# Gated cross-attention layer on one core: another order in the first units of the second phase, and Q and K kept in DRAM in another layout

## What is computed

```python
x = x + tanh(g_xattn) * xattn(layernorm(x), ctx, mask, bias, ...)
x = x + tanh(g_ffn)  * ffn(layernorm(x), ...)

def xattn(h, kv, mask, bias, ln_weight, w_q, w_k, w_v, w_out):
    n = rmsnorm(h) * ln_weight
    q, k, v = n @ w_q.T, kv @ w_k.T, kv @ w_v.T      # 4096 columns each: 32 heads of 128
    s = softmax(where(mask, einsum(q, k) + bias, -inf))   # by batch and head, 128 x 128
    return h + (einsum(where(mask, s, 0), v)) @ w_out.T   # 4096 -> 512

def ffn(y, ...):   # base product 512 x 512, router with 15 outputs, 8 LoRA experts of rank 16
```

## Time and profile before

| | |
|---|---|
| Median of 3 runs | 874.24 us (872.16 to 874.72) |
| Profiled execution | 874.5 us, its span 872.7 us |
| TensorE busy | 840.9 us (96%) |
| VectorE busy | 661.0 us (76%) |
| ScalarE busy | 490.8 us (56%) |
| GpSimd busy | 488.0 us (56%) |
| DMA queue of SyncE | 214.13 MB, 75.7% of 16 engines over the span |
| Mean granted TensorE clock | 0.986 |
| qk_units stores | 128 of 512 KB, 3.2 us to landing (median) |
| qk_units loads | 64 of 1,024 KB, 7.5 us to landing (median) |

### The profile page before, as it was taken

One profiled execution on the slowest core, in us unless ns is written; L12 is line 12 of the kernel. 1 busy time (PEld: TensorE's weight loads), 2 busy tenths in 40 slices (PEclk: granted clock), 3 DMA queues, 4 the chain that ended last, 5 costly groups with the idle time before them and its releaser, 6 DMA issues.

```text
span 872.7 us, 14037 instructions
## 1 busy us (share of the span) xinstructions
PE 840.9 (96%) x4212; PEld 711.0 (81%) x4212; DVE 661.0 (76%) x1172; ACT 490.8 (56%) x1185; POOL 488.0 (56%) x352
## 2 busy tenths in 40 slices
PE   6999999999999998699999999999999999998898
PEld 5887888778888887587888888888888888886786
DVE  6888777886776566466777788988878888798564
ACT  5566666666676654445555555555555555555210
POOL 0353633645456632565766666666666666766522
PEclk9999999999999999899999999999999999998899
DMA  8876777669777795878898888898889889885001
GB/s 293 298 273 244 272 267 262 256 254 359 303 272 281 276 331 177 253 244 265 247 263 267 259 265 259 253 260 250 250 257 261 250 261 250 275 256 175 5 25 73
DMA packets 155393, 214.73 MB, mean 246 GB/s; under 512 B 10960, under 2 KB 109392, under 8 KB 154960
## 3 DMA queue, kind: packets, MB, share of 16 engines
q1 hardware_dynamic: 155344, 214.13, 75.7%
HBM read 128.11 MB, written 85.98 MB: 245 GB/s over the span
## 4 chain that ended last, share of the span: by engine, by line
PE 63%; DVE 13%; DMA 12%; issue 3%; SPq 3%; ACT 3%; POOL 1%; DVEq 0%; ACTq 0%; POOLq 0%
DMA p_rows<-p_blocks 7%; PE Sb L1429 4%; PE Sb L1431 4%; PE Sb L1430 4%; PE Ab L1600 3%; PE Sb L1576 3%; PE Vb L1420 3%; SPq L349 3%; PE Vb L1422 2%; PE Vb L1421 2%; PE Ob L1420 2%; PE Ob L1421 2%; PE Ob L1422 2%; PE Kb L1420 2%; DVE unit_out L959 2%
## 5 line engine op out<-in xcount | busy, mean ns | idle before, releaser
L498 POOL TENSOR_TENSOR w_lo<-w_raw,w_hi 128x1280 fp32r<-128x1280 f32 (+1 forms) x29 | 84.8, 2924 | 121.8 <-ACT w_hi L646 121.8
L542 POOL TENSOR_TENSOR a_rest<-small_a,A_hi 128x512 f32<-128x512 f32 x64 | 83.0, 1297 | 120.0 <-ACT small_a L774 120.0
L780 ACT ACTIVATE p_exp<-s_sb,negmax 128x128 f32<-128x128 f32 x256 | 99.0, 388 | 12.0 <-DVE negmax L1114 11.5
L535 POOL TENSOR_TENSOR bm<-bias,maskneg 128x512 f32<-128x512 f32 x64 | 83.4, 1304 | 19.6 <-DVE s_sb L1120 11.9
L646 ACT ACTIVATE A_hi<-Ab 128x512 fp32r<-128x512 f32 x64 | 38.1, 595 | 96.9 <-PE Ab L1601 96.9
L547 POOL TENSOR_TENSOR P_hl<-pT,P_hl 128x512 fp32r<-128x512 f32 x64 | 83.4, 1302 | 5.0 <-ACT P_hl L646 5.0
L1600 PE MATMUL Ab<-P_hl,V_hi 128*128 128x256 f32 x256 | 65.4, 333 | 15.6 <-POOL P_hl L547 11.4
L646 ACT ACTIVATE U<-Sb 128x512 f32<-128x512 f32 x90 | 53.6, 600 | 41.6 <-PE Sb L1431 41.0
L646 ACT ACTIVATE w_hi<-w_raw 128x512 fp32r<-128x512 f32 (+2 forms) x67 | 60.2, 903 | 22.9 <-PE Kb L1431 7.2
L1429 PE MATMUL Sb<-t_hi,w_lo 128*128 128x512 f32 x180 | 70.5, 392 | 1.2 <-ACT U L646 1.2
L1431 PE MATMUL Sb<-t_hi,w_hi 128*128 128x512 f32 x180 | 70.1, 389 | 0.0
(11 more groups left out here) (300 smaller groups left out, 2705.4 us busy)
## 6 DMA issues: line engine op xcount, KB each, us to landing
qk_units<-unit_out SPq DMA_DIRECT2D x128, 512.0 KB, 3.2
qk<-qk_units SPq DMA_DIRECT2D x64, 1024.0 KB, 7.5
p_rows<-p_blocks SPq DMA_DIRECT2D x64, 256.0 KB, 3.2
pT<-p_rows SPq DMA_DIRECT2D x256, 64.0 KB, 3.7
w_raw<-wqk SPq DMA_DIRECT2D x31, 512.0 KB, 4.2
v_raw<-wv SPq DMA_DIRECT2D x32, 256.0 KB, 4.5
o_raw<-wo SPq DMA_DIRECT2D x32, 256.0 KB, 4.9
stage<-ctxT SPq DMA_DIRECT2D x8, 256.0 KB, 6.1
```

The source lines that it names most:

```text
L498: pool.tensor_tensor(w_lo[:, n % 2, first:5, :], w_raw[:, n % 2, first:5, :], f32(w_hi[:, n % 2, first:5, :]), ALU.subtract).then_inc(w1_l ...
L535: pool.tensor_tensor(bm[:, :, :], bias4[:, q, :, :], maskneg[:, b:b + 1, :].broadcast_to([P, HU, S]), ALU.add).then_inc(bm_done, 1)
L542: pool.tensor_tensor(a_rest[:, :, :], small_a[:, :, :], f32(A_hi[:, r, :, :]), ALU.subtract).then_inc(a_rest_done, 1)
L780: last = act.activation(p_exp[:, i, :], s_sb[:, i, :], ACT.Exp, bias=negmax[:, i:i + 1], accum_out=rowsum[:, i:i + 1])
```

## The change

1. `qk_units` becomes (2·GROUPS, P, BH, 2·HU, 2·S): the batch stands ahead of the columns. A unit's load reads one run of 8 KB per partition instead of eight of 1 KB; a store writes four runs of 1 KB per partition instead of one of 4 KB.
2. SyncE, `first_units`: the loads of units 3, 4 and 5 move ahead of stores and loads of blocks. The V weights' pieces 0 to 2 of group 1 are issued together at its end.
3. SyncE, `group`: V's pieces are issued in units 1 to 4 of a group instead of 2 to 5, the output weights' pieces in units 5, 6, 7 and 0 instead of 6, 7, 0 and 1.
4. ScalarE, `step`: the exponentials go ahead of the weight conversions. In group 0 the V weights' pieces are converted in units 4, 5, 6 and 6 instead of 3 (ahead of unit 4), 4, 5 and 6; GpSimd alike. ScalarE's list for units 1 to 3 has P's high half of unit 0 ahead of V's of unit 2, and the exponentials of unit 3 ahead of V's high half of unit 3.
5. VectorE: V_lo of unit 0 goes ahead of the normalisation of unit 1.
6. TensorE: scores 3 go ahead of V of units 2 and 3, and P·V 0 ahead of V of unit 4.

```diff
--- before.py
+++ after.py
@@ -321,7 +321,7 @@
                 g, p, half = n % G, i % 2, i // 2
                 head = HU // 2 * (g % 2) + p
                 sp.wait_ge(unit_lo_done[i], n + 1)
-                sp.dma_start(qk_units[2 * (g // 2) + half, :, 2 * head + n // G, :, :],
+                sp.dma_start(qk_units[2 * (g // 2) + half, :, :, 2 * head + n // G, :],
                              f32(unit_out[:, i, :]).rearrange("p (b k) -> p b k", b=BH)).then_inc(st[i], 16)
 
             def load_wv(g, q, k):
@@ -354,8 +354,9 @@
                 sp.dma_start(bias4[:, q, :, :], bias[g, :, :, :]).then_inc(ld_bias, 16)
 
             def load_unit(g, b):
-                sp.dma_start(f32(qk[:, b % 2, :, :, :]).rearrange("p h a k -> p (h a) k"),
-                             qk_units[2 * g + b // BH, :, :, b % BH, :]).then_inc(ld_qk[b % 2], 16)
+                sp.dma_start(f32(qk[:, b % 2, :, :, :]).rearrange("p h a k -> p (h a k)"),
+                             qk_units[2 * g + b // BH, :, b % BH, :, :].rearrange("p c k -> p (c k)")).then_inc(
+                                 ld_qk[b % 2], 16)
 
             sp.dma_start(w_raw[:, 0, A11:S1, :], wqk[0, :, 0:2, :]).then_inc(ld_w0[0], 16)
             for k in (B11, B21, B12, B22):
@@ -411,21 +412,21 @@
                     sp.wait_ge(st[i], 16 * (G + 2))
                 sp.wait_ge(scores_done, 1)
                 load_unit(0, 2)
+                sp.wait_ge(scores_done, 2)
+                load_unit(0, 3)
                 store_blocks(0, 0)
                 load_blocks(0, 0)
-                sp.wait_ge(scores_done, 2)
-                load_unit(0, 3)
                 store_blocks(0, 1)
-                load_blocks(0, 1)
                 sp.wait_ge(scores_done, 3)
                 load_unit(0, 4)
+                load_blocks(0, 1)
+                sp.wait_ge(scores_done, 4)
+                load_unit(0, 5)
                 store_blocks(0, 2)
                 load_blocks(0, 2)
                 sp.wait_ge(m_done[4], J(JOBS - 1))
-                load_wv(1, 1, 0)
-                sp.wait_ge(scores_done, 4)
-                load_unit(0, 5)
-                load_wv(1, 1, 1)
+                for k in range(3):
+                    load_wv(1, 1, k)
 
             def group(g, q):
                 first, last = (isinstance(g, int) and g == n for n in (0, GROUPS - 1))
@@ -439,12 +440,12 @@
                         sp.wait_ge(scores_done, B * g + b + 1)
                         load_unit(g + (b + 2) // B, (b + 2) % B)
                     load_blocks(*before)
-                    if 2 <= b <= 5 and not last:
-                        load_wv(g + 1, 1 - q, b - 2)
-                    if b >= 6 and not last:
-                        load_wo(g + 1, 1 - q, b - 6)
-                    if b < 2 and not first:
-                        load_wo(g, q, b + 2)
+                    if 1 <= b <= 4 and not last:
+                        load_wv(g + 1, 1 - q, b - 1)
+                    if b >= 5 and not last:
+                        load_wo(g + 1, 1 - q, b - 5)
+                    if b == 0:
+                        load_wo(g, q, 3)
                     if b == (4 if first else 1) and not last:
                         load_bias(g + 1, 1 - q)
                     if first and b > 3 and b < 7:
@@ -572,8 +573,11 @@
                     bias_and_mask(g + 1, 0, 1 - q)
                 if b < 3 and not first:
                     split_wo_lo(g, q, b + 1)
-                if not last and 3 <= b <= 6:
-                    split_wv_lo(g + 1, 1 - q, b - 3)
+                if first and b == 6:
+                    split_wv_lo(1, 1, 2)
+                    split_wv_lo(1, 1, 3)
+                elif not last and 3 <= b <= 6:
+                    split_wv_lo(g + 1, 1 - q, b - 4 if first else b - 3)
                 if not last and b == 7:
                     split_wo_lo(g + 1, 1 - q, 0)
                 if last and b == 3:
@@ -606,7 +610,6 @@
             bias_and_mask(0, 3, 0)
             probs_lo(0, 0)
             bias_and_mask(0, 4, 0)
-            split_wv_lo(1, 1, 0)
             for b in range(4, B):
                 step(0, b, 0)
             with pool.Fori(0, GROUPS // 2 - 1) as pair:
@@ -807,10 +810,14 @@
                     small_attention(t - 4)
                 v_evict_hi(t, b)
                 probs_hi(t - 3, (b - 3) % 4, B // 2 * g + (b - 1) // 2)
+                exponentials(t)
                 if b < 3 and not first:
                     split_wo_hi(g, q, b + 1)
-                if not last and 3 <= b <= 6:
-                    split_wv_hi(g + 1, 1 - q, b - 3)
+                if first and b == 6:
+                    split_wv_hi(1, 1, 2)
+                    split_wv_hi(1, 1, 3)
+                elif not last and 3 <= b <= 6:
+                    split_wv_hi(g + 1, 1 - q, b - 4 if first else b - 3)
                 if not last and b == 7:
                     split_wo_hi(g + 1, 1 - q, 0)
                 if last and b == 3:
@@ -819,7 +826,6 @@
                 if last and b == 4:
                     act.wait_ge(ld_loraB, 16)
                     late_high(w_loraB_hi, loraB_raw)
-                exponentials(t)
                 if last and b == 7:
                     act.wait_ge(ld_base, 16)
                     late_high(w_base_hi[:, 0, :], base_raw[:, 0, :])
@@ -904,11 +910,10 @@
 
             v_evict_hi(1, 1)
             exponentials(2)
+            probs_hi(0, 0, 1)
             v_evict_hi(2, 2)
-            probs_hi(0, 0, 1)
+            exponentials(3)
             v_evict_hi(3, 3)
-            exponentials(3)
-            split_wv_hi(1, 1, 0)
             for b in range(4, B):
                 step(0, b, 0)
             with act.Fori(0, GROUPS // 2 - 1) as pair:
@@ -1245,10 +1250,10 @@
                     unit_lo(R22, n - 1, C22)
                     unit_lo(R21, n - 1, X[(n - 1) % 2])
                     c12(n - 1)
+                    v_evict_lo(0, 0)
                     normalise(1, 1)
                     transpose_blocks(1)
                     scores(2)
-                    v_evict_lo(0, 0)
                     unit_lo(R12, n - 1, C12)
                     break
                 if PLAIN < n < JOBS - 1:
@@ -1667,10 +1672,16 @@
             v_half(0, 0, 0, 0, 1)
             m3(JOBS - 1)
             scores(2, 0, 2)
-            for b in (1, 2, 3):
+            v_half(1, 0, 1, 0, 0)
+            v_half(1, 0, 1, 0, 1)
+            scores(3, 0, 3)
+            for b in (2, 3):
                 v_half(b, 0, b, 0, 0)
                 v_half(b, 0, b, 0, 1)
-            for b in range(3, B):
+            apply_probs(0, 0)
+            v_half(4, 0, 4, 0, 0)
+            v_half(4, 0, 4, 0, 1)
+            for b in range(4, B):
                 step(0, b, 0)
             with pe.Fori(0, GROUPS // 2 - 1) as pair:
                 for k in range(2):
@@ -1803,7 +1814,7 @@
     nc = bacc.Bacc("TRN2", target_bir_lowering=False, num_devices=1, dynamic_dma_scratch_size=1024)
     args = [nc.dram_tensor(n, given[n].shape, mybir.dt.from_np(given[n].dtype), kind="ExternalInput").ap()
             for n in _INPUTS]
-    args.append(nc.dram_tensor("qk_units", (2 * GROUPS, P, 2 * HU, BH, 2 * S), F32, kind="Internal").ap())
+    args.append(nc.dram_tensor("qk_units", (2 * GROUPS, P, BH, 2 * HU, 2 * S), F32, kind="Internal").ap())
     args.append(nc.dram_tensor("p_rows", (2, P, Q32, HU * 32), F32, kind="Internal").ap())
     args.append(nc.dram_tensor("out", (P, B, D), F32, kind="ExternalOutput").ap())
     build(nc, *args)
```

## The result

The changed kernel takes **867.45 us** (median of 5 runs, 867.03 to 868.4; 874.24 us before). Timed side by side the ratio is 0.9937, with a 95% interval of 0.9921 to 0.9954: 5.5 us faster. The forecast was 860.1 us, a gain of 14.1 us. The sign holds and the time lies in the range, but half the gain isn't there. In the profiled execution (span 865.6 us, mean clock 0.992) the distance from the start of scores 2 to that of scores 63 is 453.04 us (332.51 to 785.55); before it is 460.21 us (331.82 to 792.03). So the seam gave 7.2 us, not 14.1. From scores 63 to the end of the span it is 80.05 us for 80.67.

What follows compares the result with a forecast made beforehand. TensorE was taken to be busy nearly throughout, with time to win only where the phases meet and at the ends. 874.2 − 14.1 (seam) + 0.5 (stores) − 0.5 (tail) = 860.1 us; forecast 857 to 863, range 855 to 869 us.

Steps and rivals of the forecast that it cites:

- the seam: Where the first phase meets the second, 320 to 415 us: waits and slow clock cost 16.0 us, 14.1 to be won.
- TensorE's order: At the seam, scores 3 and P·V 0 go earlier: idle of 0.9 and 1.0 us, scores 5 near 352.1 us.
- Left at the seam: 0.9 + 1.0 = 1.9 us: TensorE's waits before scores 3 and P·V 1 were all that would remain, too short to cost clock.
- SyncE's order: Unit loads pass block stores: unit 0's lands near 332.5, unit 2's is back at 344.8, blocks still ahead of need.
- The conversions: V weight splits moved in group 0: five GpSimd operations of 1.3 us in a unit of 7.32 us, called covered.
- Rival 1: The seam keeps a stall: block stores land 4 us later than counted, P·V 1 or 2 waits 3 us; 865 us, chance 0.16.
- Layout, the stores: First phase: 1 KB packets at 48 ns, DMA share near 0.82, jobs still 9.5 us apart; 0.5 us lost from 200 us on.
- Rival 2: Stores bind the first phase: slower from 64.7 ns a packet, 894 us at 70 ns, chance 0.07; 3 to 10 us lost, 0.09.
- Layout, the loads: A unit's load in 8 KB runs takes 1.2 us less queue time; nobody waits for it in steady state.
- The tail: TensorE's 2.38 us wait for A_lo at 798.30 shrinks with less queue: 0.5 us won, up to 3 us.

Runs made afterwards that it cites:

- splits_first_6: The changed kernel with ScalarE's two V weight conversions of unit 6 of group 0 put ahead of that unit's exponentials: 867.15 us, ratio 0.9931 to the kernel before.
- ext2_split_in_unit_5: ext2_blocks_again with piece 2 of the next group's V weights split in unit 5 instead of unit 6: 860.22 us, ratio 0.9855 to the kernel before.
- order_only: The changed kernel with the old DRAM layout of Q and K put back: 867.71 us, ratio 0.9934 to the kernel before.
- ext2_old_layout: ext2_blocks_again with the old DRAM layout of Q and K: 864.93 us, ratio 0.9911 to the kernel before.
- ext2_blocks_again: The changed kernel with two p_blocks buffers and, in group 0, SyncE's other transfers issued ahead of the block loads; a repeat run: 862.31 us, ratio 0.9877.
- two_blocks: The changed kernel with two p_blocks buffers, so a transpose waits for the store before last: 867.80 us, ratio 0.9933 to the kernel before.
- tail_order: The changed kernel with, after the last group, P's low half earlier on GpSimd and A_lo ahead of x1 on VectorE: 868.67 us, ratio 0.9967.
- extras_early: The changed kernel with SyncE, in units 4 to 7 of group 0, issuing its other DMAs ahead of the block loads: 862.86 us, ratio 0.9899.

## Why the prediction was half right

- **TensorE's order: right, stamp by stamp, as far as it went.** Scores 3 waited for 0.73 us (0.9), P·V 1 for 1.17 us (1.0), and scores 5 started at 353.27 (352.1). The step that failed is the one behind it: "Left at the seam: 0.9 + 1.0 = 1.9 us". I walked the chain as far as scores 5 and took the old steady state from there. The units behind were short of it by 1.25 + 1.36 + 2.42 us (before P·V 2, P·V 3 and V of unit 8), 0.20 us at 435.05 and 1.7 us of clock, 6.9 us in all, which is the gap between 14.1 and 7.2.
- **SyncE's order: the covers held, the counts behind them didn't, and they weren't the whole question.** The loads of unit 0's blocks could be issued at 334.93, not near 332.5, and the store of unit 2's blocks was back at 348.66, not at 344.8: 2.4 and 3.9 us later than counted. TensorE never waited there for P_hl, but VectorE waited for its buffer. I asked when ScalarE would want the blocks, not when VectorE would want its buffer back. The rows were there: the store of 343.08 in the earlier trace rows was away for 6.2 us, and 6.2 and some 2 us for loads exceed the 7.32 us of a unit. Before, as I read it, the wait of 7.36 us hid this. The trace before agrees as far as it goes: the stores of 364.54 and 373.44 are 8.9 us apart too, but the transposes of 363.75, 370.44 and 379.44, behind the long wait, stand for no store. No run shows it by itself. The two executions with the shorter round and both buffers show the price, 4.4 to 5.3 us, the spared fall of the clock included.
- **The conversions: "covered" failed.** Five GpSimd operations of 1.3 us do fit into 7.32 us as a sum; but two of them can't start before exponentials that are late, and end 2.42 us too late for V of unit 8. A sum of durations is no cover; a start time is needed too. In the changed kernel's trace the term is 2.42 us and the 1.7 us of clock behind it; moving the splits won nothing there (splits_first_6) and 2.1 us in the faster version (ext2_split_in_unit_5).
- **Rival 1 is what came**, in form (a stall kept at the seam, by stores of blocks that land late) and nearly in price: 865 us with 0.16 of chance, for 867.45 measured. Its condition, stores back 4 us later than counted, is nearly what the store of unit 2's blocks did (3.9 us). But I had P·V wait for P_hl in one unit for 3 us; it was A_lo, in two units beyond the one forecast, and v_lo in another, so that the price came out near is in part luck. I argued against it from ScalarE's margins, the wrong reader.
- **Layout, the stores: right.** 49 ns for 48 taken, a DMA share of 0.80 for 0.82, jobs 9.52 us apart. Rival 2 is excluded. ScalarE waited for stores for 2.8 us in all, for 0.8 us, while TensorE shows one wait of 0.17 us there (at 218.01). The 0.5 us taken for the first phase compare with 0.7 (332.51 − 331.82), but starts of scores 2 scatter over 331.5 to 333.3 us among the versions with these stores, so nothing is shown.
- **Layout, the loads: too low.** "In steady state nobody waits for it" wasn't contradicted, but I gave the shorter load 0.44 us at the seam. Between order_only and the changed kernel the layout is worth 0.3 us of time, which is nothing that can be told, between ext2_old_layout and ext2_blocks_again 2.6: it pays where the units run at their 7.3 us.
- **The tail: 0.6 us for 0.5, by luck, if at all.** The changed kernel's second execution has 78.82 us from scores 63 to the end for the first one's 80.05, so 0.6 us lie within the scatter. The wait for A_lo fell from 2.38 to 1.13 us as reasoned, and a wait for P_hl went from 2.12 to 5.14 us without a loss at the end that shows.

On the stores' price, an estimate from the fixed cost of about 3 cycles per packet in the Trainium skill (DMA: Bandwidth & Descriptors, "Why small descriptors are slow (HBM only)") has four packets of 1 KB cost 7% more than one of 4 KB. The trace of the changed kernel doesn't agree: 4 × 49 = 196 ns against 158, 24% more.

## What to carry to other kernels

Behind a stall that is removed, look for loops and not only for what is next: here a store's landing (5.4 us) and the issue of what SyncE has behind it (3.4 us) made a round of 8.8 us against units of 7.32, and a single buffer tied VectorE to it. Add up each such round, and compare it with the new period, before a gain is written down. Loosen the link that sets the round first: the second buffer alone was worth nothing, SyncE's order 3.3 to 3.8 us, and the buffer on top of it at most some 2 us more. A local repair elsewhere (the place of two splits) may pay only afterwards: one such edit won 0 us before, another 2.1 us after. For an engine that issues in order, what doesn't depend on the awaited landing belongs ahead of the wait.

## What the runs showed of the hardware

- Packets of 1 KB written to DRAM cost 49 ns of queue time each (120 to 121 us, changed kernel), nearly the same as the 48 ns of reads the earlier trace rows.
- A store of 256 KB took 3.8 us to land at 326.86, 5.4 us with a unit's load issued right behind it (352.04 to 357.48), and 7.2 us with one right ahead of it (341.50 to 348.66). No run moves the load alone, so what it costs the store isn't shown. SyncE took 0.38 to 0.57 us to issue most of these DMAs, and 1.88 us for one at 361.15 in two_blocks.
- TensorE's clock fell to 1.2 GHz behind waits of 1.76 and 2.18 us (order_only), 1.85 us (before, at 401.50), 1.86 us (splits_first_6), 2.01 us (tail_order), 2.42 us (changed), 2.49 us (ext2_old_layout) and 2.54 us (two_blocks). It stayed at 2.4 GHz behind 1.98 us (ext2_old_layout) and 1.92 and 1.87 us (extras_early). So the length of a wait alone doesn't tell whether the clock falls. A fall cost 1.7 us (0.83 over 10 us, changed kernel) or 3.4 us (0.66 over 10 us, ext2_old_layout).
